# A half-height MLP chunk filled to 128 rows, its activation made one bank earlier, and the rotation placed ahead of the result's addition

## The reference, cut to what matters

```
h   = rms(x) * (1 + scale_mlp) + shift_mlp
mlp = (silu(h @ w1) * (h @ w3)) @ w2        # 256 -> 704 -> 256
x2  = x + gate_mlp * mlp                    # input of the graph layer
y   = x2 + relu(output of the graph layer)  # the result
q   = rope(rms(q)); k = rope(rms(k))        # of a later block of sequences
```

## Time and profile before

| | us |
|---|---|
| median of 3 runs (1387.53 to 1390.21) | 1388.95 |
| the profiled execution | 1389.65 |
| its span in the trace | 1387.1 |
| PE busy | 1322.3 (95%) |
| PE weight loads (PEld) | 1227.1 (88%) |
| DVE busy | 1184.9 (85%) |
| ACT busy | 888.7 (64%) |
| POOL busy | 716.9 (52%) |

### The profile page before, as it was taken

How to read it: one execution, slowest core, us unless ns; L and a number is a source line. 1 busy time by engine, 2 the same in 40 slices (tenths; PEclk the granted TensorE clock), 3 DMA queues, 4 the chain that set the end, 5 groups by cost and what they waited for, 6 DMA issues and landing times.

```text
span 1387.1 us, 51521 instructions
## 1 busy us (share of the span) xinstructions
PE 1322.3 (95%) x20276; PEld 1227.1 (88%) x20276; DVE 1184.9 (85%) x2065; ACT 888.7 (64%) x1784; POOL 716.9 (52%) x676
## 2 busy tenths in 40 slices
PE   4579999999999999999999999999999999999985
PEld 4478999999999999999999999999999999999985
DVE  5667998898889889888988998898899889889763
ACT  4546666667666666766666676666667666666542
POOL 0235555545655554565555456555545655554442
PEclk9789999999999999999999999999999999999997
DMA  7001111001111100111110011111000111100100
GB/s 245 30 24 31 46 44 44 20 31 35 43 43 43 43 21 31 35 43 43 43 43 23 31 32 43 43 43 43 24 31 32 43 43 43 43 28 24 31 22 9
DMA packets 49827, 56.19 MB, mean 41 GB/s; under 512 B 4352, under 2 KB 47744, under 8 KB 49792
## 3 DMA queue, kind: packets, MB, share of 16 engines
q1 hardware_dynamic: 48944, 53.86, 12.1%
q10 hardware_dynamic: 848, 1.84, 0.4%
HBM read 47.03 MB, written 8.65 MB: 40 GB/s over the span
## 4 chain that ended last, share of the span: by engine, by line
PE 90%; issue 1%; DVE 1%; ACT 0%; POOL 0%; ACTq 0%; DVEq 0%
PE psum L486 51%; PE psum L622 5%; PE psum L728 4%; PE psum L758 4%; PE psum L792 4%; PE psum L607 4%; PE psum L775 3%; PE psum L806 3%; PE psum L587 2%; PE psum L696 2%; PE psum L570 2%; PE psum L631 1%; PE psum L534 1%; PE psum L526 1%; PE psum L541 0%
## 5 line engine op out<-in xcount | busy, mean ns | idle before, releaser
L1318 POOL TENSOR_TENSOR gl<-gf,gh 128x512 fp32r<-128x512 f32 x96 | 124.5, 1297 | 254.2 <-ACT gh L926 254.2
L486 PE MATMUL psum<-nh,w_lo 128*128 128x256 f32 x704 | 182.4, 290 | 0.1
L486 PE MATMUL psum<-nh,w_hi 128*128 128x256 f32 x704 | 176.7, 281 | 0.0
L1318 POOL TENSOR_TENSOR nl<-xn,nh 128x512 fp32r<-128x512 f32 x64 | 100.3, 1568 | 124.4 <-ACT nh L864 124.4
L486 PEld LDWEIGHTS psum<-nh,w_hi 128*128 128x128 f32 x704 | 133.1, 189 | 0.0
L486 PEld LDWEIGHTS psum<-nh,w_lo 128*128 128x128 f32 x704 | 132.5, 188 | 0.5 <-issue 0.5
L1384 POOL TENSOR_TENSOR e<-e,inv 128x640 f32<-128x640 f32 x64 | 82.0, 1281 | 88.2 <-DVE inv L1274 88.2
L486 PE MATMUL psum<-nl,w_hi 128*128 128x256 f32 x704 | 115.4, 282 | 0.0
L926 ACT ACTIVATE gh<-gf 128x512 fp32r<-128x512 f32 x96 | 60.3, 628 | 61.6 <-DVE gf L1202 60.9
L486 PEld LDWEIGHTS psum<-nl,w_hi 128*128 128x128 f32 x704 | 97.4, 188 | 0.0
L486 PE MATMUL psum<-qkv_lo,nh 128*128 128x512 f32 (+1 forms) x256 | 88.0, 355 | 3.7 <-ACT nh L864 2.8
(11 more groups left out here) (186 smaller groups left out, 4451.5 us busy)
## 6 DMA issues: line engine op xcount, KB each, us to landing
adj<-in_adj SPq DMA_DIRECT2D x32, 440.0 KB, 3.3
x_in<-in_x SPq DMA_DIRECT2D x32, 256.0 KB, 2.6
xn<-in_xT SPq DMA_DIRECT2D x32, 256.0 KB, 3.5
x_res<-in_xT SPq DMA_DIRECT2D x32, 256.0 KB, 3.6
out_T<-y SPq DMA_DIRECT2D x32, 256.0 KB, 2.2
e<-in_adaln ACTq DMA_DIRECT2D x2, 512.0 KB, 5.1
stage<-in_qkv SPq DMA_DIRECT2D x2, 384.0 KB, 4.8
pT<-in_w SPq DMA_DIRECT2D x2, 384.0 KB, 6.2
```

Source lines behind the costliest of these rows:

```text
L486: last = nc.tensor.matmul(out, lhsT, rhs, start=start and i == 0, stop=stop and i == len(terms) - 1)
L1318: return nc.gpsimd.tensor_tensor(out, full, hi.bitcast(F32), ALU.subtract)
```

## The change

1. Chunk 5 is made together with chunk 4 of w1 in z_ps; u_ps holds only chunk 4 of w3. ACT takes one tanh of both. DVE makes the half chunk in two instructions of 64 rows (activation, then product), the other chunk in two of 128 rows.
2. The host repeats the last 64 rows of w2 instead of putting 64 zero rows ahead of them. A new ACT step half_high copies the half chunk's gf, rounded, into rows 0 to 63 of gl's last chunk, whose rows 64 to 127 hold its low part. So one matmul with 128 rows multiplies high and low part at once, by w_lo and by w_hi: two for each output instead of three.
3. rope moves from the head of DVE's list to its end, as (3, "rope", ...), ahead of `out`.

```
 ORDER "DVE":
-        (2, "rope", 0), (2, "rope", 1), (0, "mlp_down", 0), (1, "mixT", 0), ...
+        (0, "mlp_down", 0), (1, "mixT", 0), ...
-        (3, "rope_scale", 0), (0, "out", 0),
+        (3, "rope_scale", 0), (3, "rope", 0), (3, "rope", 1), (0, "out", 0),
 ORDER "Activation":
-        (2, "rope_scale", 0), (0, "mlp_split", 2), (1, "mixT", 0), (0, "x2_split", 0),
+        (2, "rope_scale", 0), (0, "mlp_split", 2), (0, "half_high", 0), (1, "mixT", 0), (0, "x2_split", 0),
 PE mlp_up:
                 if 2 * n + 1 == MC - 1:
-                    chunks = {"w1": [(0, "w1", MC - 2)], "w3": [(0, "w3", MC - 2), (1, "w1", MC - 1)]}
+                    groups = [[(z, 0, "w1", MC - 2, True, False), (z, 1, "w1", MC - 1, False, True)], [(u, 0, "w3", MC - 2, True, True)]]
 PE mlp_down:
+                wait(pe, half_hi, m, 1)
                 for o in both:
-                    for i, (w, a) in enumerate(((wl["w2"], gh), (wh["w2"], gh), (wh["w2"], gl))):
-                        last = nc.tensor.matmul(down_ps[:, o, :], w[half, MC - 1, out_chunks[o]], a[half, MC - 1, :],
-                                                start=False, stop=o == DC - 1 and i == 2, tile_position=(HALF, 0))
+                    last = linear(down_ps[:, o, :], high_terms("w2", out_chunks[o], gl, [MC - 1]), False, o == DC - 1)
 ACT:
+            def half_high(m, n):
+                wait(act, g_lo, m, MC // 2)
+                nc.scalar.activation(gl[0:HALF, MC - 1, :], gf[HALF:, 1, :], ACT.Copy).then_inc(half_hi.sem, 1)
 DVE mlp_up, n == 2:
-                    nc.vector.scalar_tensor_tensor(gf[:, 0, :], th[:, 0, :], 1.0, z_ps[n][:, 0, :], ALU.add, ALU.mult)
-                    wait(dve, z_tanh, m, n + 2)
-                    nc.vector.scalar_tensor_tensor(gf[HALF:, 1, :], th[0:HALF, 1, :], 1.0, u_ps[n][0:HALF, 1, :],
-                                                   ALU.add, ALU.mult).then_inc(z_silu.sem, 1)
-                nc.vector.tensor_tensor(gf[:, :, :], gf[:, :, :], u_ps[n], ALU.mult).then_inc(g_done.sem, 1)
+                    nc.vector.scalar_tensor_tensor(gf[HALF:, 1, :], th[0:HALF, 1, :], 1.0, z_ps[n][0:HALF, 1, :],
+                                                   ALU.add, ALU.mult).then_inc(half_silu.sem, 1)
+                    nc.vector.scalar_tensor_tensor(gf[:, 0, :], th[:, 0, :], 1.0, z_ps[n][:, 0, :], ALU.add, ALU.mult)
+                    wait(dve, half_silu, m, 1)
+                    nc.vector.tensor_tensor(gf[HALF:, 1, :], gf[HALF:, 1, :], z_ps[n][HALF:, 1, :], ALU.mult).then_inc(z_silu.sem, 1)
+                    wait(dve, z_silu, m, n + 1)
+                    wait(dve, z_done, m, 2 * n + 2)
+                    nc.vector.tensor_tensor(gf[:, 0, :], gf[:, 0, :], u_ps[n][:, 0, :], ALU.mult).then_inc(g_done.sem, 1)
```

More of the change, by code:

```diff
@@ L89 @@
     "DVE": [
-        (2, "rope", 0), (2, "rope", 1), (0, "mlp_down", 0), (1, "mixT", 0), (1, "proj", 0), (0, "row_mask", 0),
+        (0, "mlp_down", 0), (1, "mixT", 0), (1, "proj", 0), (0, "row_mask", 0),
         (0, "edge_masks", 0), (2, "score_max", 0), (2, "score", 0), (1, "norm1_squares", 0), (2, "score_max", 1),
@@ L649, in mlp_up @@
                 wait(pe, normed_hi[1], m, 1)
-                chunks = {"w1": [(c, "w1", 2 * n + c) for c in range(2)], "w3": [(c, "w3", 2 * n + c) for c in range(2)]}
+                z, u = z_ps[n], u_ps[n]
+                groups = [[(z, 0, "w1", 2 * n, True, False), (z, 1, "w1", 2 * n + 1, False, True)],
+                          [(u, 0, "w3", 2 * n, True, False), (u, 1, "w3", 2 * n + 1, False, True)]]
                 if 2 * n + 1 == MC - 1:
-                    chunks = {"w1": [(0, "w1", MC - 2)], "w3": [(0, "w3", MC - 2), (1, "w1", MC - 1)]}
@@ L654, in mlp_up @@
-                for name, out in (("w1", z_ps[n]), ("w3", u_ps[n])):
-                    if (n, name) == (0, "w1"):
+                    groups = [[(z, 0, "w1", MC - 2, True, False), (z, 1, "w1", MC - 1, False, True)], [(u, 0, "w3", MC - 2, True, True)]]
+                for i, group in enumerate(groups):
+                    if (n, i) == (0, 0):
                         wait_free(pe, m, (normed[0], 2, 1), (q1_kept, -1, 2))
-                    elif (n, name) == (0, "w3"):
+                    elif (n, i) == (0, 1):
@@ L664, in mlp_up @@
                         wait_free(pe, m, (mix_normed, 1, 2), (z_silu, 0, 1))
-                    elif (n, name) == (2, "w3"):
+                    elif (n, i) == (2, 1):
                         wait_free(pe, m, (pT1_a, -1, 1), (biased1, -1, 4), (shifted_s, 1, 2))
-                    for c, w, j in chunks[name]:
-                        linear(out[:, c, :], high_terms(w, out_chunks[j], nh[1], both), c == 0, False)
-                    if name == "w1":
+                    for out, c, w, j, start, stop in group:
+                        linear(out[:, c, :], high_terms(w, out_chunks[j], nh[1], both), start, False)
@@ L670, in mlp_up @@
+                    if i == 0:
                         wait(pe, normed_lo[1], m, 1)
-                    for c, w, j in chunks[name]:
-                        last = linear(out[:, c, :], low_terms(w, out_chunks[j], nl[1], both), False, c == chunks[name][-1][0])
+                    for out, c, w, j, start, stop in group:
+                        last = linear(out[:, c, :], low_terms(w, out_chunks[j], nl[1], both), False, stop)
                     last.then_inc(z_done.sem, 1)
@@ L676, in mlp_down @@
                 first_use(m, "w2")
-                half = slice(HALF, P)
                 if n == 0:
@@ L915, in mlp_up @@
                 wait(act, z_silu, m, n)
[L916 to L921 removed]
+                nc.scalar.activation(th[:, :, :], z_ps[n], ACT.Tanh, scale=0.5).then_inc(z_tanh.sem, 1)
             def mlp_split(m, n):
```

24 lines of the change are left out of this document (10 added, 14 removed).

## The result

| | before | changed |
|---|---|---|
| median, us | 1388.91 (4 runs, 1387.53 to 1390.21) | 1403.96 (4 runs, 1400.70 to 1404.20) |
| profiled execution | 1389.65 | 1404.20 |
| its span | 1387.1 | 1402.4 |
| period in the loop | 40.42 | 40.89 |
| from the 30th x2 to the end of the span | 106.5 | 108.4 |

The changed kernel is slower: ratio 1.0094, 95% interval 1.0077 to 1.0111. The forecast was 1396.5, 7.5 us too low. Its direction and its two costs were right; both costs are larger than forecast, and so is the end of the program. Lines of the changed kernel are three higher from the product on (x2 L1211, the addition L1288, gl L1321), the rotation is L1141.

What follows compares the result with a forecast made beforehand. It took the path through x2, not PE, as the bound: 29 x 0.30 = +8.7 us, less 1.1 in the first and last blocks, +7.6 in all, giving 1396.5 us; range 1388 to 1401, likeliest case 1392.5 to 1400.

Steps and rivals of the forecast that it cites:

- its two costs: On the path to x2, per block: a later product, +0.07 us at gl, and x2's wait for the addition, +0.23.
- x2's wait for the addition: On DVE, x2 directly behind the addition it waits for starts at gl + 1.90 instead of 1.67 us: +0.23 per block.
- the product: On DVE, three instructions become four, spaced 0.43, 0.43, 0.53: g_done 0.25 us later, gl's end 0.07 later per block.
- the end: In the last block, and partly block 30, x2 waits for PE, so PE's 0.4 us is won: -1.1 with the first.
- The bound: In the self step, the path DVE, POOL, PE through x2 ends last, balanced with PE's work to under 0.1 us.
- The rival that PE sets the period: The matmuls saved are kept, 0.4 to 0.57 us in each of 30 blocks: 1372 to 1377 us; chance 0.07.
- One sign: In the self step, a visible PE wait of 0.4 us or more ahead of the low row sums.
- ACT and half_high: Two tanh become one of 0.59 us; gh starts 0.04 after g_done; the copy half_high delays nothing queued behind it on ACT.
- PE's net saving: In the down projection, 0.57 us saved by fewer matmuls, less the wait for half_high: about 0.4 us per block.
- Plain spacing, the first rival: The product's four pieces start without the partition hold: +0.03 us per block, total 1388.7 us; chance 0.14.
- The loop's sum: Later product plus x2's wait, 0.07 + 0.23 = +0.30 us per block, 29 blocks: +8.7 us.
- the rival "worse than forecast": Each own wait costs 0.15 us and half_high comes too late: +0.40 us per block, above 1400 us; chance 0.08.

Runs made afterwards that it cites:

- e3: Kernel before with only the shorter down projection (repeated w2 rows, half_high, four full-row matmuls); period 40.42 us, ratio 1.0037.
- e14: e3 with two more matmuls in the half chunk's down projection; period 40.43 us, ratio 1.0011.
- e8: e2 with the product reordered: full activation, half activation, full product, half product; period 40.36 us, ratio 1.0000 to the kernel before.
- e7: Changed kernel with a fixed gate address in x2, the first four sequences' gate for all blocks; period 40.75 us, ratio 1.0083 to the kernel before.
- e5: Changed kernel with the result's addition between the two rotations, one instruction ahead of x2; period 40.57 us, ratio 1.0046 to the kernel before.
- e11: The changed kernel run again, nothing altered; period 40.90 us, ratio 1.0113 to the kernel before.
- e4: Changed kernel with x2 as the last entry of DVE's list, before the loop's branch; period 40.87 us, ratio 1.0130 to the kernel before.
- e6: Changed kernel with x2's product in its own tile, so DVE need not wait for the addition; period 40.56 us, ratio 1.0038 to the kernel before.
- e1: Kernel before with only the rotation moved ahead of the result's addition; period 40.77 us, ratio 1.0088.
- e2: Changed kernel with the rotation back at the head of DVE's list; period 40.56 us, ratio 1.0073 to the kernel before.
- e13: Changed kernel with two more matmuls in the half chunk's down projection; period 40.89 us, ratio 1.0128 to the kernel before.
- e9: e8 with ACT's high part of the second product one place earlier; period 40.22 us, ratio 0.9973 to the kernel before.

## Why the prediction was right or wrong

**Where the missing time lies.** The span grew by 15.3 us and not by 7.6. Three terms of the sum were off: x2's wait for the addition (0.32 instead of 0.23 per block, 2.6 us in 29), the product (0.14 instead of 0.07, 2.0 us) and the end (+1.9 instead of -1.1, 3.0 us).

**The bound: right.** PE passes the self step 3.70 to 3.73 us after x2 (medians of all kernels), whether it starts the row sums at 2.69 or 2.43. Fewer matmuls (e3) and more (e14) both leave the period. The rival that PE sets the period fell. One sign came out otherwise: instead of 0.4 us or more ahead of the low row sums, PE waits 0.23 ahead of the high ones, for ACT's nh, and 0.13 ahead of the low ones. The prediction had left nh out; the total is near what it said, and the passage is the same.

**ACT and half_high: right.** One tanh fewer frees ACT; the one that is left starts 0.14 us ahead of DVE's L1130, as forecast (627.47 against 627.61). gh starts 0.04 after g_done, and the copy into gl delays nothing in the path. The last four matmuls start at 638.37, 0.05 after that copy's end. PE's net saving was mis-sized, 0.26 us (1.29 - 1.03) instead of 0.4: the wait for the copy is about as forecast, but the first matmul behind it is followed after 0.23 us (638.37 to 638.60) and not after 0.12. Nothing hangs on it, since the self step swallows it either way.

**The product: right in mechanism, mis-sized.** Forecast +0.25 at g_done and +0.07 at gl; measured +0.31 and +0.14, so twice the forecast where it counts. The pieces are spaced 0.45, 0.43, 0.55 instead of 0.43, 0.43, 0.53, and the first starts 0.03 after its predecessor instead of 0.02. Small as it is, the error of 0.06 goes through in full, because ACT's slack of 0.17 had already absorbed what it could. Plain spacing, the first rival, fell. The Trainium skill ("VectorE: DVE Perf Modes", "Two Vector instructions with no wait between them") says that a change of quadrant holds the next instruction until the earlier ones are done; e8's rows agree.

**x2's wait for the addition: right in mechanism, 0.09 us too small.** Forecast: start at gl + 1.90, from dependent pairs at 0.12 to 0.15. Measured: gl + 1.99, 0.24 after the addition's end in the loop. The step that failed is taking one price for all own waits, from pairs that have only one sequencer instruction between the two. Pairs at 0.03 stand in the same trace and were not read. The gap goes by what the sequencer still has to do once the first is done: 0.03 with nothing in between, 0.10 to 0.15 with one instruction (an event semaphore in e7, a register operation in both pairs that the forecast used), 0.24 with the two that x2 has, as it waits for relu_done and down_done and its gate's address is computed. With a fixed address the gap is 0.10 (e7, and the blocks outside the loop). Of the whole 0.32 (from 0.08 before the end to 0.24 after), 0.18 is the wait and 0.14 the register operation behind it. The Trainium skill, "VectorE: DVE Perf Modes", section "The DRAIN you can't avoid", reports a semaphore as free after each of its copies. Here an own wait right behind its producer is not; with an instruction in between (e5) it is, since the sequencer does its part while that one runs.

**The loop's sum.** 0.14 + 0.32 = 0.46 per block in place of 0.07 + 0.23 = 0.30. Over 29 periods the trace gives 1189.55 - 1176.07 = +13.5 us, instead of +8.7.

**The end: wrong in sign.** I expected -1.1, since x2 waits for PE in the last block. The 30th x2 to the last does take 69.69 us instead of 71.33, but in e3, which has the same saving on PE, it takes 71.24, so that isn't PE's gain shown. Most of it is the last distance, 33.86 instead of 35.12; it is 33.85 to 33.90 in e11, e4, e6 and e7 as well, but 35.18 in e1 and 35.33 in e2, so it comes only where the rotation's new place and the stacked chunk stand together (not in e13, with 36.95), and that stays unexplained. And from the last x2 to the end of the span it takes 38.7 instead of 35.2: together +1.9. The stage view of the changed kernel, 4 us each from the last x2 on:

```profile
1363.70:1367.70 4.00, 1.59 (x11) 1.45 (x12) 0.87 (x3) 0.83 (x2) 2.78 (x4) 1.00 0.20 68
1367.70:1371.70 4.00, 3.07 (x15) 2.55 (x13) 1.68 (x4) 1.77 (x4) 0.49 (x1) 0.52 0.00 0
1371.70:1375.70 4.00, 4.00 (x20) 4.00 (x20) 1.26 (x4) 0.00 (x0) 0.78 (x1) 0.50 0.00 0
```

and of the kernel before, at the same places:

```profile
1351.90:1355.90 4.00, 1.56 (x7) 1.56 (x8) 0.76 (x2) 0.83 (x2) 2.77 (x4) 0.82 0.14 48
1355.90:1359.90 4.00, 3.07 (x18) 2.68 (x16) 1.80 (x4) 1.38 (x4) 0.00 (x0) 0.76 0.00 0
1359.90:1363.90 4.00, 4.00 (x27) 4.00 (x26) 1.26 (x4) 0.39 (x2) 1.27 (x1) 0.67 0.02 4
```

The third last figure is PE's granted clock. In the first stretch it is higher than before (1.00 against 0.82), in the next two about 0.50 (1.2 GHz) where before had 0.76 and 0.67 on average, and in the third fewer matmuls are done, 20 against 27. Over the whole stretch from the last x2 to the end it is 0.69 against 0.78. All 13 profiles with the repeated rows of w2 have an end of 107.0 to 111.3 us, the three without 105.3 to 106.5. That is a pattern of one profiled execution each: e3, the new down projection alone, has it, and e14, with the same number of full-row matmuls as there were half-row ones, keeps it. That the down projection causes it, and by what in it, is not shown.

Together -0.1 + 13.5 + 1.9 = +15.3 us of span (-0.1 is the first x2); the forecast was +7.6. The time thus falls where the rival "worse than forecast" put it, but not by its means: the copy sets no part of the path through x2 (its 64 rows are done at 638.32, aoh starts at 639.67 after a wait for PE), and own waits of 0.15 would give 0.1 less than the 0.24 measured.

## What to carry to other kernels

Put at least one instruction between a producer and a consumer on the same engine that waits for it, above all where the consumer has several waits and an address computed in a loop: 0.32 us per iteration here, nothing with one instruction in between. Take the price of a wait from a pair with the same sequencer instructions in between, not from any dependent pair. Before removing work from the busiest engine, look for a point that it passes at a fixed distance from another engine's work; if there is one, shorten that path (here e8 and e9), or the saving turns into waiting.

## What the runs showed of the hardware

- A DVE instruction with no wait starts 0.08 us before its predecessor's end; with a change between partition 0 and 64, 0.01 to 0.04 after it.
- With a wait for its predecessor it starts 0.03 after the end where no sequencer instruction stands between them, 0.10 to 0.15 after it with one (event semaphore, register operation), and 0.22 to 0.24 after it with an event semaphore and then a register operation that computes its address.
- A wait for the instruction before last cost nothing beyond that (e5, e8, and the half chunk's product in the changed kernel, 634.85 to 634.86).
- Whichever DVE instruction with two SBUF inputs began beside POOL's gl ended about 0.55 us after it: the addition in the kernel before (1.58 us instead of 0.68), the rotation in e5 (1.23 us, to 636.05; gl ended at 635.50). Reordering them moves the delay and does not hide it.
- From the last x2 to the end the same instructions took 33.9 to 39.6 us in the 16 profiles; in the one of before the granted clock averaged 0.78 there, in the changed kernel's 0.69.
